# A gated cross-attention and FFN block on one Trainium2 core: FFN statistics one block earlier, first normalising on GpSimd, row loads in four pieces, two ScalarE roundings in other places

## The chip, the cores and the metric

The kernel runs on one core of a Trainium2 chip. The metric is the device time of one execution in microseconds (us). Three executions of the kernel before took 907.96, 905.91 and 907.97 us; the median is 907.96 us.

The engines are named as the profile names them: PE (TensorE, matrix products; PEld is its weight load), DVE (VectorE), ACT (ScalarE), POOL (GpSimd), and SP (SyncE), whose queue SPq issues nearly all DMAs. Each engine works through its own list of instructions in order and waits on semaphores.

## The reference

```python
x = x + tanh(g_xattn) * attention(layernorm(x), ctx, ctx, Wq, Wk, Wv, Wo)   # 16 heads of 32, causal mask
x = x + tanh(g_ffn)   * ffn(layernorm(x), w_gate, w_up, w_down)
# attention: softmax(q k^T / sqrt(32) + mask) v, then Wo; x is (2, 2048, 512), ctx is (2, 77, 512)
# ffn: (silu(x w_gate^T) * (x w_up^T)) w_down^T, hidden size 1536, integer weights / 127
# layernorm has no gain or bias, eps 1e-5
```

All of it is float32. The kernel splits each float32 operand of most products into a rounded high part (made by ACT) and a low part (the rest, made by DVE or POOL by a subtraction) and adds the cross products.

## The kernel before

**Stage 1, attention.** The 4096 rows are 8 blocks (n = 0 to 7) of 4 tiles (t = 0 to 3) of 128 rows. `step(n, ...)` exists once for each engine and states its order in a block. For tile t, PE computes the scores `scores(n, t)` in two halves; DVE's `shift` takes the maxima (L1029, L1037), subtracts (L1032) and scales (L1039); ACT takes exponentials, `exp0` (L767) for the first half and `exp1` (L774, eight pieces) for the second; DVE makes the denominators (L1052, L1054, L1058); POOL's `probabilities` (L571) multiplies by them. PE transposes the result, `p(t, 0)` to `p(t, 2)` (L1494), ACT rounds each transpose to its high part (L745) and DVE takes the low part (L998), which frees the PSUM bank. The second half of `scores(n, t+1)` waits for `exp1(n, t)`. `values` (L1460, psum<-pT,V) and the output projection `o(t)` (L1460, psum<-wo,aT) of the block before, and the query product `q(m)` of the next one (psum<-xT,wq), stand between these steps; `q(m)` may begin once DVE has freed one of two banks, by `q_low` (L1014). DVE's `residual` (L1064) ends a tile; SP writes it to the tensor `x_mid` (L404).

In block 0 alone, SP scatters the values of both batches into `v_full` with 24 small DMAs (L429), ACT rounds batch 0 in `v_high(0)` and batch 1 in `v_high(1)` (L736), and POOL and DVE make the low parts. ACT goes on to block 1 when `v_split[1]` has come, POOL's low part of batch 1.

For block n+1, SP spreads the factor `rstd` over partitions by two DMAs, one behind the other (`spread_rstd`: L359 writes `rs_row`, L365 reads `rsb`); POOL then scales (`x_scale`, L557) and takes the low parts (L563).

**To stage 2.** The FFN reads `x_mid` in 4 pairs of blocks, each 8 tiles of 128 x 512 in `x2`. For the first pair DVE computes mean and variance, `stats2` (L1116, L1118): 4 tiles in block 6 and 4 tiles in block 7. There, at the same place `st(t)` of each t: st(0) and st(1) do two tiles each, st(2) and st(3) call `normalise2` (L1124) for four tiles each. POOL's `rstd_ahead` (L651, L653) gives the factors. PE transposes the eight tiles in four `turn`s (L1572): B11 and B12 in block 7 after `o(3)`, ahead of `p(3, 0)`; B22 and B21 among the last `values`. ACT and DVE turn these into seven left factors of a Strassen product.

SP loads `x2` for the first pair as two DMAs of 1 MB (`load_x2`, L369), one before `residual(6)` and one after it. `residual(6)` also holds the `x_res` loads (L395) and `spread_rstd(7)`.

**Stage 2, FFN.** Each pair p has MH = 12 slices m of the hidden size (i = 12p + m). A slice is seven products of 4 matmuls: PE runs p1(i), p2(i), p4(i-1), p6(i), p3(i-1), p5(i), p7(i), 28 matmuls (L1705). After slice m = 6, PE runs the first half of the down products (`down`, 96 matmuls, L1755), and the second half after m = 11. Weights come in a ring of three slots: at the end of p3(i), SP issues `load_w(i+3)` (L387, 896 KB). In the first pair it first waits until DVE has taken the largest weight of the slot (L1345). Where other loads stand behind `load_w`, they and their waits delay the next `load_w`, since SP works in order.

ACT in slice m runs `snap1(i)` (L905, copy of p1, which p6(i) waits for), tanh2, tanh1, `snap2(i)` (L911), `h_high(i-1, 0)`, `snap3(i)` (L917), `h_high(i-1, 1)` (L937). `h_high(i-1, 1)` waits for DVE's `hidden2(i-1)` (L1332). POOL takes the low parts in `h_low` (L680). In the first pair POOL also converts the down weights (`convert`, L686), two of six pieces after each of `h_low(0)` to `h_low(2)`.

Other loads of SP in stage 2: pieces 4 and 5 of the down weights at m = 0 of the first pair; `acc` (the rows to which the result is added, 2 x 1 MB) at m = 2 of the first pair, behind a wait for all six conversions (L481), and at m = 0 of the others (L456); `x2` of the next pair (2 x 1 MB) at m = 3.

Of the kernel before, what the change touches and what calls it, by code (L numbers as in the profile page):

```python
# [5 lines left out]
def flamingo_gated_block(  # L6
# [31 lines left out]
    ALU = mybir.AluOpType  # L38
# [3 lines left out]
    P = 128  # L42
# [9 lines left out]
    TT = 4  # L52
# [55 lines left out]
    with ctx:  # L108
# [28 lines left out]
        rstd2 = sb("rstd2", [P, PT])  # L137

# [125 lines left out]
        acc_in = sem("acc_in")  # L264
        bn2_done, stats2_ready = sem("bn2_done"), sem("stats2_ready")
        var2_eps, rstd2_ready = sem("var2_eps"), sem("rstd2_ready")
        x2_normed = sem("x2_normed")
# [69 lines left out]
        def _(sp):  # L337
# [29 lines left out]
            def load_x2(q, j):  # L367

                sp.dma_start(x2[:, j * TT:(j + 1) * TT, :], mid_f[2 * q + j]).then_inc(x2_in[j], 16)  # L369
# [70 lines left out]
            load_x2(0, 0)  # L440
            residual(NB - 2, spread=True, keeps=((True,), (False,)))
            load_x2(0, 1)
# [9 lines left out]

            def load_rows(p):
                sp.wait_ge(out_done, 16 * PT * p)
                for j in range(2):
                    sp.dma_start(acc[:, j * TT:(j + 1) * TT, :], mid_f[2 * p + j]).then_inc(acc_in, 16)  # L456
# [7 lines left out]
            def pair(p):  # L464
                for m in range(MH):
                    i = MH * p + m
                    sp.wait_ge(p3_full, i + 1)
                    if p == 0 and m < HH:
                        sp.wait_ge(w_max_done, m + 1)
                    if p == NP - 1 and m >= HH:  # L470
                        sp.wait_ge(w_max_done, m + 1)
                    if i + 3 < MH * NP:
                        load_w(i + 3)
                    if p == 0 and m == 0:
                        for j in (4, 5):
                            sp.wait_ge(rd_used, j - 3)
                            load_down(j)
                    if p == 0 and m == 2:
                        sp.wait_ge(rd_used, HH)
                        for j in range(2):  # L480
                            sp.dma_start(acc[:, j * TT:(j + 1) * TT, :], mid_f[j]).then_inc(acc_in, 16)  # L481
                    if p > 0 and m == 0:
                        load_rows(p)
                    if p + 1 < NP and m == 3:
                        sp.wait_ge(xb_full, nth(TURNED, p, B21))
                        for j in range(2):
                            load_x2(p + 1, j)
                for t in range(PT):
                    sp.wait_ge(m_free, M_P2 + 16 * p + 9 + t)
                    sp.dma_start(out_f[2 * p + t // TT, :, t % TT, :], acc[:, t, :]).then_inc(out_done, 16)  # L490
# [21 lines left out]
        def _(pool):  # L512
# [201 lines left out]
        def _(act):  # L714
# [83 lines left out]
            def step(n, first, query):  # L798
# [31 lines left out]
                if first:  # L830
# [4 lines left out]
                    v_high(1)  # L835
# [4 lines left out]
                    q(2)  # L840
                    p(3, 0)
# [97 lines left out]
            def pair(p, more):  # L939
                last = MH * p + MH - 1  # L940
                for m in range(MH):
                    i = MH * p + m
                    snap1(i)
                    if m:
                        tanh2(i - 1)
                        tanh1(i - 1)
# [4 lines left out]
                    if m:  # L951
                        h_high(i - 1, 1)
# [27 lines left out]
        def _(dve):  # L980
# [130 lines left out]
            def stats2(i, t):  # L1111

                at = TT * (i % 2) + t
                if t == 0:
                    dve.wait_ge(x2_in[i % 2], 16 * (i // 2 + 1))
# [36 lines left out]
            def step(n, first, query, ahead):  # L1152
# [181 lines left out]
            def result(p, h, t):  # L1334
                dve.wait_ge(m_full, M_P2 + 16 * p + PT * h + t + 1)
                if h == 0:
                    dve.wait_ge(acc_in, 32 * (p + 1))
# [118 lines left out]
        def _(pe):  # L1456
# [88 lines left out]
            def turn(q, j):  # L1545
# [4 lines left out]
                pe.wait_ge(x2_normed, PT * q + TT * (half_of + 1))  # L1550
# [300 lines left out]
```

## Time and profile before

| | |
|---|---|
| median of 3 executions | 907.96 us |
| the profiled execution | 910.43 us, of which 908.6 us are its span |
| PE busy | 865.1 us, 95% of the span |
| DVE, ACT, POOL busy | 643.1, 435.8, 427.5 us |
| DMA | 129.53 MB, mean 143 GB/s |
| stage 1, stage 2 | to about 403 us, from about 403 us |

In the timeline a row is: start in us, time in us, engine, line, operation, output <- inputs, shapes, count of instructions, and in brackets the engine's idle time just before and what ended it. Neighbours of the same kind are merged into one row. A matmul lasts longer than the distance to the next (they are pipelined), so the pace of PE is read from the time of a whole row. PEclk is the share of full clock that PE was granted: 1.00 is 2.4 GHz, 0.50 is 1.2 GHz.

### The profile page before, as it was taken

The page shows a single profiled execution, that of the slowest core. Times are in us where ns is not written, and L with a number is a line of the kernel's source. Part 1 is how long each engine was busy: PE and PEld are TensorE (multiplying, and loading weights), DVE is VectorE, ACT ScalarE, POOL GpSimd, SP SyncE. Part 2 cuts the span into 40 slices and gives each one's busy share as a digit, 9 for nine tenths or more (in the row PEclk, how much of TensorE's full clock was granted, in tenths as well). Part 3 has the DMA queues.
Part 4 walks back from the last instruction along what each step waited for, and adds up shares of the span by engine and source line. Part 5 has one row for each costly group of instructions (what it writes and reads, how often), then busy time and mean ns, then how long its engine had stood idle before and what let it go on. Part 6 is the DMA issues. An engine that isn't in the chain of part 4 may idle for free.

```text
span 908.6 us, 12903 instructions
## 1 busy us (share of the span) xinstructions
PE 865.1 (95%) x4089; PEld 712.7 (78%) x4089; DVE 643.1 (71%) x1090; ACT 435.8 (48%) x1130; POOL 427.5 (47%) x362
## 2 busy tenths in 40 slices
PE   4978999999999999899899999999999999999997
PEld 2757888888888887678688888888888878888876
DVE  3776868685868778759668747687567677477682
ACT  2565656555565656436406536246355165362450
POOL 5364767675767663146414524334534145242240
PEclk9999999999999999899999999999999999999999
DMA  6425373655546350526804327324256043262212
GB/s 199 151 61 177 114 232 128 195 163 161 176 153 218 116 207 12 203 73 235 307 0 144 135 86 275 126 82 157 93 202 233 2 158 119 97 219 79 82 41 94
DMA packets 61589, 129.53 MB, mean 143 GB/s; under 512 B 8416, under 2 KB 21216, under 8 KB 61536
## 3 DMA queue, kind: packets, MB, share of 16 engines
q1 hardware_dynamic: 61248, 128.85, 41.5%
q8 instruction: 29, 0.48, 0.2%
q14 instruction: 24, 0.20, 0.1%
q10 hardware_dynamic: 288, 0.00, 0.0%
HBM read 100.72 MB, written 27.80 MB: 141 GB/s over the span
## 4 chain that ended last, share of the span: by engine, by line
PE 76%; DVE 7%; POOL 5%; ACT 4%; issue 3%; SPq 3%; DMA 2%; ACTq 0%; POOLq 0%; DVEq 0%
PE psum L1705 30%; PE psum L1460 24%; PE psum L1755 18%; POOL xs L557 3%; PE psum L1494 3%; SPq L429 2%; POOL e L571 1%; DMA ring<-w_var 1%; POOL hT L680 1%; PE psum L1572 1%; ACT e L774 1%; DVE pT L998 1%; DVE x L1124 1%; DMA wq_stage<-wq_t 1%; ACT pT L745 1%
## 5 line engine op out<-in xcount | busy, mean ns | idle before, releaser
L1705 PE MATMUL psum<-xv,ring 128*128 128x512 f32 x1344 | 310.3, 392 | 5.1 <-DMA ring<-w_var 3.6
L1705 PEld LDWEIGHTS psum<-xv,ring 128*128 128x128 f32 x1344 | 252.1, 189 | 60.8 <-issue 4.2
L680 POOL TENSOR_TENSOR hT<-th,hT 128x512 fp32r<-128x512 f32 x48 | 85.1, 1772 | 221.0 <-ACT hT L937 221.0
L1755 PE MATMUL psum<-w_d,hT 128*128 128x512 f32 x768 | 177.6, 390 | 1.2 <-POOL hT L680 0.7
L1755 PEld LDWEIGHTS psum<-w_d,hT 128*128 128x128 f32 x768 | 143.6, 188 | 32.5 <-POOL hT L680 2.0
L571 POOL TENSOR_TENSOR e<-e,rden 128x616 f32<-128x616 f32 x64 | 77.9, 1217 | 115.2 <-DVE rden L1054 83.7
L1460 PE MATMUL psum<-xT,wq 128*128 128x512 f32 x384 | 96.5, 405 | 3.0 <-POOL xT L563 2.9
L1460 PE MATMUL psum<-wo,aT 128*128 128x512 f32 x384 | 95.1, 398 | 0.5 <-DVE aT L1014 0.5
L1340 DVE SCALAR_TENSOR_TENSOR acc<-psum,gate_ffn,acc 128x512 f32<-128x512 f32 x64 | 47.6, 749 | 65.5 <-PE psum L1755 65.4
L905 ACT ACTIVATE a<-psum 128x512 f32<-128x512 f32 x48 | 28.3, 590 | 125.6 <-PE psum L1705 125.6
L1460 PEld LDWEIGHTS psum<-xT,wq 128*128 128x128 f32 x384 | 72.4, 194 | 18.3 <-POOL xT L563 3.1
L1460 PEld LDWEIGHTS psum<-wo,aT 128*128 128x128 f32 x384 | 69.9, 188 | 14.4 <-DVE aT L1014 0.8
L774 ACT ACTIVATE e<-psum,nmx 128x77 f32<-128x77 f32 x256 | 79.1, 338 | 0.2 <-DVE nmx L1039 0.2
L745 ACT ACTIVATE pT<-psum 128x512 fp32r<-128x512 f32 (+1 forms) x96 | 50.4, 533 | 45.4 <-PE psum L1494 45.4
L1460 PE MATMUL psum<-pT,V 128*128 128x512 f32 x288 | 67.9, 393 | 0.0
L680 POOL TENSOR_TENSOR hT<-c,hT 128x512 fp32r<-128x512 f32 x48 | 62.3, 1297 | 11.2 <-ACT hT L937 11.2
L1460 PE MATMUL psum<-K,qT 128*128 128x308 f32 x384 | 65.0, 313 | 2.3 <-ACT e L774 1.9
L998 DVE TENSOR_TENSOR pT<-psum,pT 128x512 fp32r<-128x512 f32 (+1 forms) x96 | 55.9, 588 | 14.3 <-ACT pT L745 13.3
L1460 PEld LDWEIGHTS psum<-pT,V 128*128 128x128 f32 x288 | 54.2, 190 | 11.0
L1460 PEld LDWEIGHTS psum<-K,qT 128*128 128x128 f32 x384 | 57.1, 188 | 7.0 <-ACT e L774 2.7
L1494 PE MATMUL psum<-ident,e 128*128 128x128 f32 x320 | 48.8, 282 | 11.3 <-DVE pT L998 10.3
L1299 DVE TENSOR_TENSOR c<-psum,a 128x512 f32<-128x512 f32 x48 | 33.0, 689 | 34.0 <-ACT a L917 34.0
(105 smaller groups left out, 1220.7 us busy)
## 6 DMA issues: line engine op xcount, KB each, us to landing
ring<-w_var SPq DMA_DIRECT2D x48, 896.0 KB, 4.8
w_var<-stage SPq DMA_DIRECT2D x12, 896.0 KB, 5.0
x_ln<-x SPq DMA_DIRECT2D x32, 256.0 KB, 4.7
x_res<-x SPq DMA_DIRECT2D x32, 256.0 KB, 6.3
x_mid<-x_res SPq DMA_DIRECT2D x32, 256.0 KB, 2.0
x<-x_mid SPq DMA_DIRECT2D x8, 1024.0 KB, 8.9
acc<-x_mid SPq DMA_DIRECT2D x8, 1024.0 KB, 8.2
out<-acc SPq DMA_DIRECT2D x32, 256.0 KB, 2.0
```

Source lines behind the costliest of these rows:

```text
L571: nc.gpsimd.tensor_tensor(e[:, t % 2, hs], e[:, t % 2, hs], rden[:, t % 2, hs].unsqueeze(2).to_broadcast([P, UH, SK]), ALU.mult).then_inc( ...
L680: nc.gpsimd.tensor_tensor(hT[:, 1, i % HH, j, :], h[:, :], hT[:, 0, i % HH, j, :].bitcast(f32), ALU.subtract).then_inc(h_lo, 1)
L745: nc.scalar.activation(dst, src, ACT.Copy).then_inc(t_hi, 1)
L774: last = nc.scalar.activation(e[:, t % 2, UH + h, :], s_bank[1][:, h // HG, (h % HG) * SK:(h % HG + 1) * SK], ACT.Exp, bias=nmx[:, t % 2, ...
L905: nc.scalar.activation(a1[:, :], psum[:, set_a[i % 2], :], ACT.Copy).then_inc(a1_done, 1)
L998: nc.vector.tensor_tensor(dst, src, hi.bitcast(f32), ALU.subtract).then_inc(t_free, 1)
L1299: nc.vector.tensor_tensor(c22[:, :], psum[:, set_c[i % 2], :], a3[:, :], ALU.add).then_inc(c22_done, 1)
L1340: nc.vector.scalar_tensor_tensor(acc[:, t, :], m_bank[t % 2][:, :], gate_ffn[:, 0:1], acc[:, t, :], ALU.mult, ALU.add).then_inc(m_free, 1)
L1460: last = nc.tensor.matmul(dst, stat, mov, start=(j == 0), stop=(j == len(terms) - 1))
L1494: last = nc.tensor.transpose(t_bank[at % 2][:, j * P:(j + 1) * P], rows[:, start:start + P], ident[:, :])
L1705: last = nc.tensor.matmul(psum[:, bank, :], stat, mov, start=start and j == 0, stop=j == len(terms) - 1, skip_group_check=not start)
L1755: last = nc.tensor.matmul(m_bank[t % 2][:, :], hT[:, a, m, t // TT, (t % TT) * P:(t % TT + 1) * P], w_d[:, HH * h + m, :], start=m == 0 an ...
```

## The change

- SP: `x2` comes in four pieces of 512 KB (2 tiles each). For the first pair all four are issued ahead of `residual(6)`. For the others one piece stands behind `load_w` at each of m = 0 to 3. `acc` also comes in four pieces, one at m = 4 and three at m = 5, each with its own semaphore; the waits for `out_done` and for the conversions move to m = 4. Pieces 4 and 5 of the down weights move from m = 0 to m = 1.
- DVE: in block 6 `st(t)` computes statistics of two tiles (8 in all); in block 7 it does nothing.
- POOL: both `rstd_ahead` stand before `probabilities(7, 0)`, and `normalise_first` (a negated mean, then four tiles by (x - mean) * rstd) stands after `probabilities(7, 0)` and after `probabilities(7, 1)`.
- ACT: `v_high(1)` moves from after `p(2, 0)` of block 0 to after `q(2)`. `h_high(i-1, 1)` moves from the end of slice i to after `snap1(i+1)`, except in slices 6 and 11, where it stays.

```diff
-            def load_x2(q, j):
-                sp.dma_start(x2[:, j * TT:(j + 1) * TT, :], mid_f[2 * q + j]).then_inc(x2_in[j], 16)
+            def load_x2(q, i):
+                sp.dma_start(x2[:, 2 * i:2 * i + 2, :], mid_f[2 * q + i // 2, :, 2 * (i % 2):2 * (i % 2) + 2, :])\
+                    .then_inc(x2_in[i // 2], 16)
+            def load_acc(p, i):
+                sp.dma_start(acc[:, 2 * i:2 * i + 2, :], mid_f[2 * p + i // 2, :, 2 * (i % 2):2 * (i % 2) + 2, :])\
+                    .then_inc(acc_in[i], 16)
...
-            load_x2(0, 0)
+            for i in range(TT):
+                load_x2(0, i)
             residual(NB - 2, spread=True, keeps=((True,), (False,)))
-            load_x2(0, 1)
             residual(NB - 1, keeps=((False,), ()))
...
-                    if p == 0 and m == 0:
+                    if p == 0 and m == 1:
                         for j in (4, 5):
                             sp.wait_ge(rd_used, j - 3)
                             load_down(j)
-                    if p == 0 and m == 2:
-                        sp.wait_ge(rd_used, HH)
-                        for j in range(2):
-                            sp.dma_start(acc[:, j * TT:(j + 1) * TT, :], mid_f[j]).then_inc(acc_in, 16)
-                    if p > 0 and m == 0:
-                        load_rows(p)
-                    if p + 1 < NP and m == 3:
+                    if p + 1 < NP and m < TT:
                         sp.wait_ge(xb_full, nth(TURNED, p, B21))
-                        for j in range(2):
-                            load_x2(p + 1, j)
+                        load_x2(p + 1, m)
+                    if m == TT:
+                        if p:
+                            sp.wait_ge(out_done, 16 * PT * p)
+                        else:
+                            sp.wait_ge(rd_used, HH)
+                        load_acc(p, 0)
+                    if m == TT + 1:
+                        for j in range(1, TT):
+                            load_acc(p, j)
...
+            def normalise_first(i):
+                c = slice(TT * i, TT * i + TT)
+                nc.gpsimd.tensor_scalar(nmean2[:, c], mv2[:, c, 0], -1.0, 0.0, ALU.mult, ALU.add).then_inc(nmean_ready, 1)
+                pool.wait_ge(nmean_ready, i + 1)
+                pool.wait_ge(rstd2_ready, i + 1)
+                for t in range(TT):
+                    at = TT * i + t
+                    nc.gpsimd.tensor_scalar(x2[:, at, :], x2[:, at, :], nmean2[:, at:at + 1], rstd2[:, at:at + 1],
+                                            ALU.add, ALU.mult).then_inc(x2_normed0, 1)
+            rstd_ahead(0)
+            rstd_ahead(1)
             probabilities(NB - 1, 0)
-            rstd_ahead(0)
+            normalise_first(0)
             probabilities(NB - 1, 1)
+            normalise_first(1)
             probabilities(NB - 1, 2)
-            rstd_ahead(1)
             probabilities(NB - 1, 3)
...
                     p(2, 0)
-                    v_high(1)
                     p(2, 1)
                     exp1(n, 3)
                     q(1)
                     p(2, 2)
                     q(2)
+                    v_high(1)
                     p(3, 0)
...
                     snap1(i)
+                    if m > 1 and m != HH + 1:
+                        h_high(i - 2, 1)
                     if m:
                         tanh2(i - 1)
...
                     snap3(i)
-                    if m:
+                    if m in (HH, MH - 1):
                         h_high(i - 1, 1)
...
                     elif query:
-                        stats2(0, t)
-                    elif t < 2:
-                        stats2(1, 2 * t)
-                        stats2(1, 2 * t + 1)
-                    else:
-                        normalise2(t - 2)
+                        stats2(t // 2, 2 * (t % 2))
+                        stats2(t // 2, 2 * (t % 2) + 1)
```

The other lines of the diff give `acc` four semaphores, let PE's first `turn`s wait for `x2_normed0`, and fit the counts of the waits.

## Rows read from the trace of the kernel before

**Rows 1.** The page: busy time by engine, with counts of instructions.

```profile
PE 865.1 (95%) x4089; PEld 712.7 (78%) x4089; DVE 643.1 (71%) x1090; ACT 435.8 (48%) x1130; POOL 427.5 (47%) x362
```

**Rows 2.** Waits of PE, whole span: engine, line, releaser: us, times, longest.

```profile
PE psum L1572 <- DVE x L1124: 3.3, 2, 2.6
```

**Rows 3.** Timeline, block 0, ACT, POOL and PE.

```profile
68.50 1.49 ACT L736 ACTIVATE V<-v_full 128x1536 fp32r<-128x1536 f32 x1 [1.88 <-DMA v_full<-v_keys]
...
74.41 3.46 POOL L600 TENSOR_TENSOR V<-v_full,V 128x1536 fp32r<-128x1536 f32 x1
...
74.61 1.08 PE L1494 MATMUL psum<-ident,e 128*128 128x128 f32 x4 [2.05 <-DVE pT L998]
75.35 4.22 PE L1460 MATMUL psum<-xT,wq 128*128 128x512 f32 x12
...
81.94 8.35 PE L1460 MATMUL psum<-pT,V 128*128 128x512 f32 x36
```

**Rows 4.** Timeline, block 6, SP, POOL, DVE, PEld and PE.

```profile
298.47 0.33 SPq L365 DMA_DIRECT2D rsb<-rs_row  x1
...
305.08 5.03 POOL L557 TENSOR_TENSOR xs<-xs,rsb 128x512 f32<-128x512 f32 x4
...
319.43 0.68 DVE L998 TENSOR_TENSOR pT<-psum,pT 128x512 fp32r<-128x512 f32 x1
...
320.17 0.36 PEld L1494 LDWEIGHTS psum<-ident,e 128*128 128x128 f32 x2
...
328.81 5.72 PE L1460 MATMUL psum<-xT,wq 128*128 128x512 f32 x24
...
329.99 0.66 DVE L1014 TENSOR_TENSOR qT<-psum,qT 128x512 fp32r<-128x512 f32 x1
```

**Rows 5.** The tile rsb from 286 to 310 us: time from issue to landing.

```profile
DMA to landing us min/median/max: 3.5/3.5/3.5
```

**Rows 6.** Timeline, block 7, POOL, DVE, PE.

```profile
344.69 1.22 POOL L571 TENSOR_TENSOR e<-e,rden 128x616 f32<-128x616 f32 x1 [7.47 <-DVE rden L1054]
...
355.73 0.69 DVE L1116 BATCH_NORM_STATS2 bn<-x 128x6 f32<-128x512 f32 x1
...
357.35 0.78 DVE L1029 TENSOR_REDUCE mx<-psum 128x8 f32<-128x616 f32 x1
...
361.55 1.22 POOL L571 TENSOR_TENSOR e<-e,rden 128x616 f32<-128x616 f32 x1 [4.93 <-DVE rden L1054]
...
368.41 3.01 PE L1460 MATMUL psum<-wo,aT 128*128 128x512 f32 x12
...
372.10 1.09 PE L1572 MATMUL psum<-ident,x 128*128 128x128 f32 x8 [0.69 <-DVE x L1124]
...
375.82 1.97 PE L1572 MATMUL psum<-ident,x 128*128 128x128 f32 x8 [2.62 <-DVE x L1124]
...
380.39 4.96 PE L1460 MATMUL psum<-pT,V 128*128 128x512 f32 x18
```

**Rows 7.** Windows: us; busy and count of PE, PEld, DVE, ACT, POOL; PEclk, DMA share, GB/s.

```profile
375.00:378.00 3.00, 2.18 (x10) 2.19 (x11) 1.89 (x3) 0.00 (x0) 0.00 (x0) 0.50 0.94 326
```

**Rows 8.** One line each: L549 (first block's normalising on POOL); L1039 on DVE.

```profile
L549 POOL TENSOR_SCALAR x_ln<-x_ln,nmean,rstd x4: 767/767/768, 10.8 to 13.0; 128x512 f32<-128x512 f32 x4
L1039 DVE TENSOR_SCALAR nmx<-mx x32: 171/172/1052, 40.8 to 367.4; 128x8 f32<-128x8 f32 x32
```

**Rows 9.** Timeline, first pair: SP, then PE.

```profile
433.72 0.45 SPq L387 DMA_DIRECT2D ring<-w_var  x1
...
443.38 8.14 PE L1705 MATMUL psum<-xv,ring 128*128 128x512 f32 x28 [3.64 <-DMA ring<-w_var]
```

**Rows 10.** Chain in order of time: a stretch of the first pair without stops.

```profile
473.29 31.75 PE psum L1705 x140
```

**Rows 11.** The tile ring, whole span: time from issue to landing.

```profile
DMA to landing us min/median/max: 4.3/4.8/12.8
```

**Rows 12.** Timeline, third pair, PE at p6 of slice 8.

```profile
731.13 3.03 PE L1705 MATMUL psum<-xv,ring 128*128 128x512 f32 x12 [0.77 <-ACT a L905]
```

More of the change, by code:

```diff
@@ L137, in flamingo_gated_block @@
         rstd2 = sb("rstd2", [P, PT])
+        nmean2 = sb("nmean2", [P, PT])
         with ExitStack() as a0:
@@ L263, in flamingo_gated_block @@
         x2_in = [sem(f"x2_in{i}") for i in range(2)]
-        acc_in = sem("acc_in")
+        acc_in = [sem(f"acc_in{i}") for i in range(4)]
         bn2_done, stats2_ready = sem("bn2_done"), sem("stats2_ready")
         var2_eps, rstd2_ready = sem("var2_eps"), sem("rstd2_ready")
-        x2_normed = sem("x2_normed")
+        x2_normed0, x2_normed, nmean_ready = sem("x2_normed0"), sem("x2_normed"), sem("nmean_ready")
         p1_full, p2_full, p3_full, p4_full, p5_full, p6_full, p7_full = (sem(f"p{i}_full") for i in range(1, 8))
@@ L451, in _ @@
                 sp.wait_ge(mid_out[t], 16 * NB)
-            def load_rows(p):
-                sp.wait_ge(out_done, 16 * PT * p)
-                for j in range(2):
-                    sp.dma_start(acc[:, j * TT:(j + 1) * TT, :], mid_f[2 * p + j]).then_inc(acc_in, 16)
             def load_down(i):
@@ L477, in pair @@
                             load_down(j)
-                    if p == 0 and m == 2:
-                        sp.wait_ge(rd_used, HH)
-                        for j in range(2):
-                            sp.dma_start(acc[:, j * TT:(j + 1) * TT, :], mid_f[j]).then_inc(acc_in, 16)
-                    if p > 0 and m == 0:
-                        load_rows(p)
-                    if p + 1 < NP and m == 3:
-                        sp.wait_ge(xb_full, nth(TURNED, p, B21))
-                        for j in range(2):
-                            load_x2(p + 1, j)
+                    if p + 1 < NP and m < TT:
+                        sp.wait_ge(xb_full, nth(TURNED, p, B21))
+                        load_x2(p + 1, m)
[8 more added lines that the diff above has]
+                            load_acc(p, j)
                 for t in range(PT):
@@ L1114, in stats2 @@
                 if t == 0:
-                    dve.wait_ge(x2_in[i % 2], 16 * (i // 2 + 1))
+                    dve.wait_ge(x2_in[i % 2], 32 * (i // 2 + 1))
                 nc.vector.bn_stats(bn2[:, at, :], x2[:, at, :]).then_inc(bn2_done, 1)
@@ L1336, in result @@
                 if h == 0:
-                    dve.wait_ge(acc_in, 32 * (p + 1))
+                    dve.wait_ge(acc_in[t // 2], 16 * (p + 1))
                 else:
@@ L1549, in turn @@
                 last_i = MH * q - 1
-                pe.wait_ge(x2_normed, PT * q + TT * (half_of + 1))
+                if q:
+                    pe.wait_ge(x2_normed, PT * (q - 1) + TT * (half_of + 1))
+                else:
+                    pe.wait_ge(x2_normed0, TT * (half_of + 1))
                 if j == B11:
```

## Prediction

> **What bounds the kernel.** I read the page first: PE is busy for 865.1 of 908.6 us [rows 1], so only two things can change the time much: where PE stands still, and where it works at a lower clock. So next the waits of PE, then the granted clock window by window, then the timeline around each wait. The wait list is misleading if read alone: it has 3.3 us for the transposes of `x2` behind normalising [rows 2], but after some stops PE is also slower for a while. Four places bear on this change.
>
> Block 0: ACT stands at `v_high(1)` until a DMA lands at 68.50, and `exp1(0, 3)`, the four `q` and `p` roundings are queued behind it [rows 3]. Block 7: two tiles of statistics stand directly in front of `shift(2)`, on which the tile's exponentials wait; later PE waits for `normalise2`, and its clock is 0.50 just after [rows 6, 7]. First pair: a weight load is issued at 433.72 behind `acc` and its wait, PE stands for 3.64 us and then takes 8.14 us for 28 matmuls [rows 9], where 140 take 31.75 us elsewhere [rows 10], that is 6.35 us for 28. Third pair: p6 of slice 8 waits 0.77 us for `snap1` [rows 12].
>
> **Block 0, `v_high(1)` moved: 3.4 us won.** ACT waited 1.88 us, from 66.62 to 68.50, and worked to 69.99 [rows 3]; without both, `p(2, 1)` and `exp1(0, 3)` come 3.3 us sooner. `v_high(1)` now fits behind `q(2)`, at about 72.7 to 74.2; POOL's low part of it, which stood behind `probabilities(0, 3)` until 74.41 [rows 3], begins no later, and nobody waits for it before block 1. PE was done with `q(2)` and `p(3, 0)` at 74.61 - 2.05 = 72.56, stood, and took 4.22 us for the 12 matmuls of `q(3)` [rows 3], where 12 take 3.01 us in block 7 [rows 6]. After, `p(3, 1)` (0.5 us) and `q(3)` (3.0 us) follow at once and end at 76.1; `p(3, 2)` and the scores, whose second half waits for DVE to free `q(3)` (ACT 0.6 us, DVE 0.7 us), let `values` begin at about 78.5 instead of 81.94 [rows 3]. If the slow pace remains, 1.2 us and one more piece of it are lost: the low end is 1.9, the high end 3.5.
>
> **Block 6, four more tiles of statistics on DVE: 1.5 us lost.** Two tiles take 357.35 - 355.73 = 1.62 us [rows 6], and four more are 3.3 us, in four places of 0.8 us. DVE has hardly a gap there. In front of `shift(2)`: the low part of `p(1, 0)` ends at 320.1, and PE's `p(1, 2)` is loaded at 320.17 [rows 4], so 0.8 us go straight to PE. `q_low(0)`, which ends at 330.65, comes behind three of the four places and is 2.5 us late, at 333.15; `q(2)`, the second half of 5.72 us from 328.81 [rows 4], would begin at 331.67 and is 0.8 late already, so it waits 0.7 us more. Behind that DVE waits for ACT and catches up. Sum about 1.5. The bounds: 0 if the chain of exponentials hides it, 3.3 if all of it shows.
>
> **Block 6, 1 MB more ahead of `rs_row`: nothing, but close.** `rsb` is issued at 298.47 [rows 4] and lands 3.5 us later [rows 5], at 302.0; POOL begins to scale at 305.08 [rows 4], so the slack is 3.1 us. Another 1 MB at the 326 GB/s of a busy window [rows 7] is 3.2 us. I take 0 and up to 1.5 us as a bound; the cover is `probabilities(6, 0)`. The three more DMA issues, each under 0.5 us of SP's time, lie inside the backlog that these bytes make.
>
> **Block 7: 5.6 us won.** On POOL, both `rstd_ahead` go into a 7.47 us gap before `probabilities(7, 0)`. `normalise_first` is 4 x 0.767 [rows 8] plus 0.2 for the mean, 3.3 us: the first lies between `probabilities(7, 0)` and `(7, 1)`, where POOL is as idle, the second in a gap of 4.93 us [rows 6], now some 1.5 us shorter, so it just fits. On DVE, `shift(2)` starts 1.5 us sooner, `shift(3)` nearly 3. PE then is the later one: `o(1)`, `p(1, 2)`, the scores, `p(2, 0)`, `p(2, 1)`, `o(2)`, `p(2, 2)`, `o(3)` run close together, and `o(3)` ends at about 370.4, not 371.4 [rows 6]. `turn` B11 needs 1.09 us, and B12, which began at 375.82 behind 2.62 us of waiting and took 1.97 us [rows 6], now follows it: 372.6. `p(3, 0)` and `p(3, 1)` end at 373.7; ACT has B11's copy (1.0 us) ahead of rounding them, PE waits 0.9 us, and `values` begins at 375.0 instead of 380.39 [rows 6], 5.4 us sooner. Its first 18 matmuls took 4.96 us [rows 6] and at 2.4 GHz would take 4.4: 0.6 more. POOL's normalising runs beside DVE's scaling of the second maxima (L1039), which is 0.17 us alone and was up to 1.05 us in blocks where POOL is busy [rows 8]; it is on the chain once, and I take off 0.4. Bounds: 2.5 if DVE's chain stays the later one and the clock falls as before; 6.5.
>
> The Trainium skill ("SBUF — State Buffer", Who interferes with whom) says that GpSimd and VectorE share a port pair that one of them holds for a whole instruction, the other blocking fully. The maximum of L1039 agrees in kind [rows 8]. By that rule a collision costs at most one 0.767 us instruction of POOL, so the block would win 5.6 + 0.4 - 0.8 = 5.2 us, and the sum would be 13.3.
>
> **First pair of stage 2: 5.4 us won.** The wait for the conversions and the 2 MB of `acc` no longer stand before `load_w(6)`. It is issued at the end of p3(3), about 431.3, and lands after about 4.8 us [rows 11], at 436; p1(6) comes at 439.7. The stop of 3.64 and the slow 8.14 - 6.35 = 1.79 go together. Pieces 4 and 5 of the down weights come one slice later: about 425, needed by POOL at 430. The row pieces stand behind `load_w` and have a slice of 6.35 us before the next: 896 + 512 KB in 6.35 us is 227 GB/s, below the 326 seen. `acc` is asked for at about 438 and 444 and used from 449. Bounds: 3.6 (the slow pace stays elsewhere) and 5.5.
>
> **`h_high`: 0.8 us won.** `snap1(8)` of the third pair no longer waits for `hidden2` behind the long DVE stretch [rows 12]. In ordinary slices p6 has 1.8 us of cover (8 matmuls) and the rounding lies in front of tanh2, which is then 0.5 us later with as much slack; POOL's low part ends 1 us ahead of the next use. Bounds 0 and 0.8.
>
> **Sum.** 3.4 - 1.5 + 0 + 5.6 + 5.4 + 0.8 = 13.7 us. Against the profiled execution, 910.43 us, this gives 896.7; that one stands 2.5 above the median of 907.96, so the predicted median is 894.3 us.
>
> **Rivals.** (a) The waits go, the clock does not come back. PE still stands for 2.9 us in block 0 and has short stops in block 7, and low stretches may fall on other work. For it: at 375 to 378 the clock was 0.50 though the stop just before was only 2.62 us [rows 6, 7], and three of my terms count on full pace. Against: the stops that preceded those stretches go. Price: 1.2 in block 0; in block 7 0.6 for the first `values`, 1.97 - 1.09 = 0.9 for B12 and some 0.5 for the `p(3, ...)` behind it; 1.8 in the first pair. That is 5.0 us, so 8.7 are won: 899.3.
>
> (b) Block 6 is dearer: all of the 3.3 us of statistics shows and `rsb` lands 1.5 us late, against 1.5 in my sum. Price 3.3 more: 897.6. For it: DVE hardly idles there, and the slack is within 0.1 us of the extra load. Against: ACT and PE have some slack of their own behind `q(2)`.
>
> (c) Slower: the row pieces hold up the ring in every pair. A load has 36 matmuls, 8.2 us, from issue to use. If pieces of 512 KB move so slowly that one is still in the queue when the next `load_w` is issued, and a load passes 8.2 us once in each of the four pairs, each costs what it cost in the first pair, 3.64 + 1.79 = 5.4 us. The win outside that pair is 8.3, so the net is 4 x 5.4 - 8.3 = 13.3 us slower, 921.3. The point from which it decides is the second stop in all: 2 x 5.4 is more than the 8.3 won elsewhere. Against it: the median landing is 4.8 us, and the one load that made PE stop stood behind 2 MB and a wait [rows 9, 11]. The Trainium skill ("DMA: Bandwidth & Descriptors", Rules for kernel authors) advises at least 1 MiB per DMA for bandwidth and so speaks for this rival; no row here shows halves to be slower than wholes.
>
> (d) The change does not do what it says: `normalise_first` lags on POOL and holds `probabilities(7, 2)`, so that block 7 gives only 2.5. Price 3.1: 897.4.
>
> **Chances.** Forecast 0.55 (891.5 to 896.5), (a) 0.15, (b) 0.13, (d) 0.10, (c) 0.03, and 0.04 for something that brings the time to within 0.3% of before, which is about what a measurement of this kernel can tell from no change (2.7 us). The range is 890.5 to 902.0: it holds the forecast, (a), (b), (d) and most pairs of them. Faster 0.93, same 0.04, slower 0.03.
>
> **What would show it.** Right: no wait of PE L1705 for the ring; no `L1572` wait for DVE; `values` of block 1 some 3.4 us sooner; stage 2 beginning about 7.5 us sooner (3.4 - 1.5 + 5.6); PEclk 1.00 between the turns and `values`, and in slice 6 of the first pair. In block 6, PE waiting for L998 or L1014 about 1.5 us. Wrong: POOL waiting for `rsb`; `probabilities(7, 2)` directly behind normalising; new low stretches of PEclk; landings of ring loads above 8 us.

## The result and the profile after

The changed kernel takes 893.96 us (median of 4 executions, 893.72 to 894.10) against 907.97 us for the kernel before on the same chip (4 executions, 905.91 to 908.66). The ratio is 0.9847, with a 95% interval of 0.9835 to 0.9859: 14.0 us less. The forecast was 894.3.

The profiled execution after took 893.84 us, that before 910.43, so the two profiles differ by 16.6 us, not 14.0. That gap turns out to matter.

The page after, busy time by engine:

```profile
span 892.0 us, 12923 instructions
PE 858.7 (96%) x4089; PEld 708.5 (79%) x4089; DVE 655.2 (73%) x1082; ACT 439.6 (49%) x1130; POOL 437.0 (49%) x372
```

PE is busy 6.4 us less for the same 4089 matmuls [rows 1]: that is pace (clock), not work. DVE is busy 12 us more, though it lost the normalising of the first pair.

Waits of PE after, whole span (engine, line, releaser: us, times, longest; the first matmuls' load and lines below 0.5 us left out):

```profile
PE psum L1509 <- DVE pT L1017: 8.4, 9, 1.3
...
PE psum L1475 <- DVE qT L1033: 0.7, 2, 0.5
```

The ring's wait and the waits of the `x2` transposes (now L1590) for DVE are not in that list. The four places, one after the other.

**Block 0.** Timeline after, ACT, then PE:

```profile
72.45 1.48 ACT L753 ACTIVATE V<-v_full 128x1536 fp32r<-128x1536 f32 x1
...
71.76 1.03 PE L1509 MATMUL psum<-ident,e 128*128 128x128 f32 x8
72.55 3.02 PE L1475 MATMUL psum<-xT,wq 128*128 128x512 f32 x12
...
77.94 2.23 PE L1475 MATMUL psum<-pT,V 128*128 128x512 f32 x9
```

`p(3, 0)` is whole, without the stop in its middle, `q(3)` takes 3.02 us, and `values` begin 4.0 us sooner than in [rows 3].

**Block 6.** POOL's scaling from 296 to 304 us after (the tile `xs`: durations in ns, first and last start):

```profile
L561 POOL TENSOR_TENSOR xs<-xs,rsb x3: 1289/1291/1292, 301.3 to 303.8; 128x512 f32<-128x512 f32 x3
```

And the timeline after, PE:

```profile
317.16 0.44 PE L1509 MATMUL psum<-ident,e 128*128 128x128 f32 x2 [0.43 <-DVE pT L1017]
...
329.32 3.02 PE L1475 MATMUL psum<-xT,wq 128*128 128x512 f32 x12 [0.49 <-DVE qT L1033]
```

POOL begins at 301.3, 3.8 us sooner than in [rows 4], so `rsb` did not hold it. PE waits for DVE's rounding of `p` and `q`, and the last rows of the block are only 2.2 us sooner: the block lost 1.6 us.

**Block 7.** Timeline after, POOL, then DVE, then PE:

```profile
354.68 3.04 POOL L680 TENSOR_SCALAR x<-x,nmean,rstd 128x512 f32<-128x512 f32 x4
357.84 1.22 POOL L575 TENSOR_TENSOR e<-e,rden 128x616 f32<-128x616 f32 x1
...
347.50 0.79 DVE L1048 TENSOR_REDUCE mx<-psum 128x8 f32<-128x616 f32 x1
353.53 0.79 DVE L1048 TENSOR_REDUCE mx<-psum 128x8 f32<-128x616 f32 x1
...
363.90 3.02 PE L1475 MATMUL psum<-wo,aT 128*128 128x512 f32 x12
366.76 1.91 PE L1590 MATMUL psum<-ident,x 128*128 128x128 f32 x16
...
371.02 4.36 PE L1475 MATMUL psum<-pT,V 128*128 128x512 f32 x18
```

A tile now takes 6.03 us (353.53 - 347.50), where it took 7.65 before (from 349.70 to 357.35 [rows 6]). Between 353.88 and 366.76 PE has no wait. Before, the same stretch had three (timeline, PE, before):

```profile
360.59 0.44 PE L1494 MATMUL psum<-ident,e 128*128 128x128 f32 x2 [0.52 <-DVE pT L998]
...
362.77 1.12 PE L1460 MATMUL psum<-K,qT 128*128 128x308 f32 x6 [0.89 <-ACT e L774]
...
368.21 0.44 PE L1494 MATMUL psum<-ident,e 128*128 128x128 f32 x2 [0.49 <-DVE pT L998]
```

Normalising is ready (357.72) long before PE turns `x2` at 366.76, both halves in one go, and `values` begin at 371.02 instead of 380.39 [rows 6]; the 18 matmuls take 4.36 us, not 4.96. Windows after, over the turns and what follows (us; busy and count of PE, PEld, DVE, ACT, POOL; PEclk, DMA share, GB/s), where [rows 7] had 0.50:

```profile
366.00:371.00 5.00, 3.72 (x31) 3.26 (x30) 2.80 (x4) 2.88 (x4) 0.47 (x1) 1.00 0.54 179
371.00:378.00 7.00, 7.00 (x37) 5.89 (x37) 4.43 (x6) 2.67 (x5) 0.00 (x0) 1.00 1.00 411
```

**First pair.** The chain in order of time after (start, us):

```profile
392.96 42.81 PE psum L1723 x188
435.77 21.77 PE psum L1773 x96
```

The timeline of SP's queue after:

```profile
433.98 0.34 SPq L394 DMA_DIRECT2D ring<-w_var  x1
434.36 1.90 SPq L375 DMA_DIRECT2D acc<-x_mid  x3
```

The three pieces of `acc` stand behind the weight load. And the tile `ring` after, from issue to landing:

```profile
DMA to landing us min/median/max: 4.4/4.6/8.2
```

All 188 up matmuls of half a pair run as one stretch, as they did before in the later pairs. The down matmuls begin at 435.77 instead of 451.52, 15.75 us sooner, where stage 2 itself begins 10.0 sooner (392.96 against 402.96): 5.75 us won inside the pair.

**Last pair.** It runs from 764.86 to 887.22, 122.36 us; before it took 121.90. Half a microsecond was lost there, which no step of the prediction has. The third pair is 1.1 us shorter (125.07 before, 123.97 now). Together the places account for the two profiles: 4.0 - 1.6 + 7.8 + 5.8 + 1.1 - 0.5 = 16.6 us.

### The profile page after: what moved, and what is told of

It reads as the page before. It is cut to its first block, busy times and chain, and to the rows that moved or that the text cites. A ratio compares the mean times of both kernels' runs of the same rounds, so it can differ in the third digit from the quotient of the medians.

```text
span 892.0 us, 12923 instructions
## 1 busy us (share of the span) xinstructions
PE 858.7 (96%) x4089; PEld 708.5 (79%) x4089; DVE 655.2 (73%) x1082; ACT 439.6 (49%) x1130; POOL 437.0 (49%) x372
## 4 chain that ended last, share of the span: by engine, by line
PE 79%; POOL 6%; DVE 6%; ACT 4%; issue 3%; DMA 1%; SPq 0%; ACTq 0%; POOLq 0%; DVEq 0%
PE psum L1723 34%; PE psum L1475 24%; PE psum L1773 18%; POOL xs L561 4%; PE psum L1509 3%; POOL e L575 2%; ACT e L791 1%; PE psum L1590 1%; ACT pT L762 1%; DMA wq_stage<-wq_t 1%; DVE pT L1017 1%; DVE den L1071 1%; POOL hT L697 1%; DVE aT L1033 1%; ACT aT L779 1%
## 5 line engine op out<-in xcount | busy, mean ns | idle before, releaser
L1319 DVE SCALAR_TENSOR_TENSOR th<-th,c 128x512 f32<-128x512 f32 x48 | 56.1, 1168 | 7.1 <-ACT th L947 4.3
L954 ACT ACTIVATE hT<-th 128x512 fp32r<-128x512 f32 x48 | 30.4, 633 | 54.2 <-DVE th L1332 54.2
```

The costliest lines, as they stand in the source:

```text
L954: nc.scalar.activation(hT[:, 0, i % HH, j, :], h[:, :], ACT.Copy).then_inc(h_hi, 1)
L1319: nc.vector.scalar_tensor_tensor(th2[:, :], th2[:, :], 1.0, c22[:, :], ALU.add, ALU.mult)\
```

## The experiments

Twelve runs, one of them (9) the kernel before again. "Before" and "after" are the two kernels of this document. Times are medians; each ratio is against the kernel before on the same chip.

**1 to 4: the parts one at a time.** Four edits of the kernel before, each taking one part of the change. My theory: the terms of the sum. The rival: the parts lean on each other, so that they do not add up.

Only `v_high(1)` moved:

```diff
                     p(2, 0)
-                    v_high(1)
                     p(2, 1)
...
                     q(2)
+                    v_high(1)
```

> The kernel before with one edit: v_high(1) of block 0 stands after q(2). My theory: ACT's wait for the last of the v_full DMAs and the rounding itself held exp1(0,3), and the slow pace of q(3) came from the stop behind it, so values of block 1 begins 3.4 to 4.0 us sooner than at 81.94 and nothing gives it back: 3.4 to 4.0 us faster. Rival: the slow pace of q(3) stays wherever the stop goes, 1.9 to 2.5 us faster. Second rival: the gain is given back at the start of stage 2, 0 to 1 us faster.

Measured: 905.71 us, 0.9978 (0.9969 to 0.9986), 2.3 us won (1.3 to 2.8), less than the 3.4 of the sum. The number is that of the first rival (1.9 to 2.5), but not for its reason: in this trace `q(3)` takes 3.00 us, so its slow pace did not stay. Experiment 9 has the reason.

Only `h_high(., 1)` moved:

```diff
                     snap1(i)
+                    if m > 1 and m != HH + 1:
+                        h_high(i - 2, 1)
...
-                    if m:
+                    if m in (HH, MH - 1):
                         h_high(i - 1, 1)
```

> The kernel before with one edit: h_high(i-1, 1) stands after snap1(i+1), as in the changed kernel. My theory: only the 0.77 us wait of p6 in slice 8 of the third pair goes: 0.8 us faster, and no other wait of L1705 appears. Rival: tanh2 that is now later delays PE in the pairs where DVE is full (first and last): same or up to 0.5 us slower.

Measured: 908.64 us, 1.0012 (1.0003 to 1.0020): 0.6 us lost by the medians (0.3 to 1.8 by the interval) where 0.8 were to be won. In its trace the third pair is 1.1 us shorter, as wanted; but the first pair is 1.0 longer and the last 0.4. Timeline of the last pair, DVE and POOL, this kernel:

```profile
858.37 0.68 DVE L1292 TENSOR_TENSOR c<-psum,a 128x512 f32<-128x512 f32 x1
858.51 1.30 POOL L680 TENSOR_TENSOR hT<-c,hT 128x512 fp32r<-128x512 f32 x1 [0.63 <-ACT hT L937]
859.15 1.20 DVE L1306 SCALAR_TENSOR_TENSOR th<-th,c 128x512 f32<-128x512 f32 x1
```

The same operation, `silu2`, grouped by line, in the kernel before (count, busy us, mean ns, idle time before):

```profile
L1304 DVE SCALAR_TENSOR_TENSOR th<-th,c 128x512 f32<-128x512 f32 x48 | 36.0, 751 | 4.6 <-ACT th L930 4.3
```

and in this one:

```profile
L1306 DVE SCALAR_TENSOR_TENSOR th<-th,c 128x512 f32<-128x512 f32 x48 | 56.0, 1168 | 7.1 <-ACT th L930 4.3
```

The earlier rounding lets POOL begin its `h_low` earlier, and it now lies across DVE's `silu2`, which reads only SBUF. That operation takes 1.20 us instead of 0.68, ending 0.5 us after POOL's; the one just before, which reads PSUM, overlaps POOL's too and still takes 0.68. The changed kernel has the same mean of 1168 ns: 48 x 0.42 is 20 us, and less the 4.5 of normalising that left and some 3 of other operations that POOL now crosses less, this is DVE's 12 us of extra busy time. The Trainium skill ("SBUF — State Buffer", Who interferes with whom) says that a DVE instruction with two SBUF inputs contends with a GpSimd instruction that reads SBUF, and that one with at most one SBUF input, outside certain modes, does not. The trace agrees on both, with 0.5 us a time for the first.

The first pair's loss is another chain. Waits of SP's queue from 383 to 450 us, this kernel:

```profile
SPq L481 <- POOL w_d L686: 8.4, 1, 8.4
```

The same of the kernel before, from 395 to 450 us:

```profile
SPq L481 <- POOL w_d L686: 7.4, 1, 7.4
```

And this kernel's wait of PE for the ring:

```profile
PE psum L1707 <- DMA ring<-w_var: 4.5, 2, 4.1
```

POOL takes `h_low` ahead of a conversion of the down weights, SP waits longer for the conversions in front of `load_w`, and the ring's wait grows from 3.6 to 4.5 us.

Only SP's queue of stage 2 (places and 512 KB pieces):

```diff
-                    if p == 0 and m == 2:
-                        sp.wait_ge(rd_used, HH)
...
+                    if p + 1 < NP and m < TT:
...
+                        load_x2(p + 1, m)
+                    if m == TT:
...
+                        load_acc(p, 0)
```

> The kernel before with the loads of stage 2 placed as in the changed kernel, in pieces of 512 KB; the first pair's x2 comes in four pieces, two of them ahead of residual(6) and two behind it, so that block 6 has the same bytes in its queue as before. My theory: the wait for the ring and the slow 28 matmuls behind it go, 5.4 us faster in the profile. Rival a: the slow pace stays, 3.6. Rival b: the ring is late in other slices, 2 us or less, or slower. Rival c: in most executions of the kernel before the stop is followed by no slow stretch, then the median moves by 3.6 only, while its profile shows what the first theory says.

Measured: 902.60 us, 0.9938 (0.9925 to 0.9950), 5.4 us won (4.5 to 6.8). Its chain in order of time:

```profile
403.00 43.14 PE psum L1710 x188
```

The stop and the slow 28 matmuls are gone together; the first pair takes 124.3 us instead of 129.8.

Only blocks 6 and 7 changed (statistics, normalising on POOL, the early `x2` loads; SP's places of stage 2 as before, but in 512 KB pieces):

> The changed kernel with v_high(1) and h_high back in their old places and the loads of stage 2 at their old places (in pieces of 512 KB): only blocks 6 and 7 are changed. By the two profiles block 6 costs 1.6 us and block 7 with the start of stage 2 wins 7.8: 6.2 us faster, with the ring's stop of 3.6 us still there. By my recorded terms 5.6 - 1.5 = 4.1 us faster. Rival: without the other parts the clock falls in block 7 all the same: 3 us or less.

Measured: 901.36 us, 0.9931 (0.9916 to 0.9946), 6.7 us won (4.9 to 7.6), against 5.6 - 1.5 = 4.1 of the sum. The second profile of the kernel before (experiment 9) has `values` of block 0 at the same time (79.39, here 79.37), so the two can be compared: stage 2 begins 6.2 us sooner here (394.33 against 400.55), and the third pair is 1.0 us shorter (124.03 against 125.00). That the third pair is shorter was not expected, since `h_high` is in its old place here. Timeline of the third pair, POOL and DVE, in the kernel before, which waits at [rows 12]:

```profile
728.09 1.29 POOL L680 TENSOR_TENSOR hT<-th,hT 128x512 fp32r<-128x512 f32 x1 [5.51 <-ACT hT L937]
728.42 1.51 DVE L1332 TENSOR_TENSOR c<-c,th 128x512 f32<-128x512 f32 x1 [0.47 <-DVE c L1325]
```

and in this one, which does not:

```profile
718.82 0.69 DVE L1345 TENSOR_TENSOR c<-c,th 128x512 f32<-128x512 f32 x1
718.86 1.81 POOL L697 TENSOR_TENSOR hT<-th,hT 128x512 fp32r<-128x512 f32 x1 [5.51 <-ACT hT L954]
```

So the wait at [rows 12] is the same kind of collision, and who comes first decides. Where POOL does (before twice, experiments 1, 2, 3 and 7), `hidden2` (L1332) takes 1.51 us; where DVE is 0.04 us ahead (after, and the other experiments), it takes 0.69 and POOL pays instead, with 1.81 for 1.29. What tips it one way or the other no run here shows. In experiments 2 and 7 POOL comes first and PE still doesn't wait: there the rounding is moved, so `snap1` no longer stands behind `hidden2`. Either is enough.

Together: 2.3 - 0.6 + 5.4 + 6.7 = 13.8, against 14.0 for the whole change. But this doesn't show that the parts add up. The microsecond of the third pair is in experiment 2 and in experiment 4, and can be won only once; the microsecond that experiment 2 lost in the first pair isn't lost in the whole change (its first pair takes 124.01 us, 0.3 less than experiment 5 without the early rounding there), where the ring's stop is gone. The parts do lean on each other, in two places that cancel.

**5: `h_high` where it helps.** In the kernel after, the early rounding at slice 8 alone, which is where [rows 12] shows its use:

```diff
-                    if m > 1 and m != HH + 1:
+                    if m == HH + 2:
                         h_high(i - 2, 1)
...
-                    if m in (HH, MH - 1):
+                    if m and m != HH + 1:
                         h_high(i - 1, 1)
```

> The changed kernel, but h_high(i-1, 1) goes back to the end of its slice everywhere except that h_high(6, 1) of each pair still stands behind snap1 of slice 8. In the changed kernel DVE's silu2 (one SCALAR_TENSOR_TENSOR with both inputs in SBUF) takes 1168 ns on average instead of 751, because POOL's low part of h now runs beside it, and the last pair, where DVE is full, takes 0.46 us longer. My theory: both go back, silu2 to 750 ns, the third pair keeps its gain: 0.3 to 0.8 us faster than the changed kernel. Rival: the last pair is longer for another reason, silu2 goes back and the time does not: within 0.2 us.

Measured: 893.84 us, 0.9846 (0.9833 to 0.9858), no different from the change. `silu2` is back at a mean of 799 ns, and the last pair takes 121.86 us, 0.5 less; but the first takes 0.3 more (188 matmuls in 43.11 us, not 42.81). DVE's time is mostly hidden, and what it cost at the end the early rounding roughly gives back in the first pair. That slice 8 still needs it is not shown: `hidden2` takes 0.69 us there in this kernel and after, as in experiment 4, which has no wait without it.

**6: the statistics of block 6 in other places.** After, with one tile per `st(t)` and the other four behind `q(1)` and `p(3, 0)` of DVE's list:

```diff
                     elif query:
-                        stats2(t // 2, 2 * (t % 2))
-                        stats2(t // 2, 2 * (t % 2) + 1)
+                        stats2(0, t)
...
                     q(1)
+                    if query and not ahead:
+                        stats2(1, 0)
+                        stats2(1, 1)
                     q(2)
                     p(3, 0)
+                    if query and not ahead:
+                        stats2(1, 2)
+                        stats2(1, 3)
```

> The changed kernel with the four added tiles of statistics of block 6 moved from st(0) to st(3) to two places where DVE waits for ACT: two behind q(1), two behind p(3, 0). My theory: what block 6 lost (1.6 us by the two profiles) was DVE's low part of p(1, 0) and its q_low(0) coming late; PE then no longer waits at these places and 1.3 to 1.6 us are won on the changed kernel, unless the statistics end too late for POOL's rstd_ahead. Rival: the loss was the later load of rsb or the clock, then nothing is won. Second rival: it moves to block 7, 0 to 0.5 us won.

Measured: 892.16 us, 0.9828 (0.9815 to 0.9841), 1.8 us better than the change. Timeline of block 6, DVE, then PE, this kernel:

```profile
328.36 0.68 DVE L1135 BATCH_NORM_STATS2 bn<-x 128x6 f32<-128x512 f32 x1
...
330.47 0.69 DVE L1033 TENSOR_TENSOR qT<-psum,qT 128x512 fp32r<-128x512 f32 x1 [0.42 <-ACT qT L779]
...
324.07 5.74 PE L1480 MATMUL psum<-xT,wq 128*128 128x512 f32 x24
```

Here DVE still idles 0.42 us behind the statistics, where it waits for ACT, and PE takes its 24 matmuls of `q(1)` and `q(2)` in one stretch, without the 0.49 us seen above. So the 1.5 us of the prediction's block 6 were real, and avoidable.

**7: who normalises.** After, with DVE normalising the first pair in block 7 (in `st(2)` and `st(3)`, as before), and all statistics in block 6:

```diff
                         stats2(t // 2, 2 * (t % 2) + 1)
+                    elif t >= 2:
+                        normalise2(t - 2)
...
-            normalise_first(0)
             probabilities(NB - 1, 1)
-            normalise_first(1)
```

> The changed kernel, but the first pair is normalised by DVE in block 7 again, at st(2) and st(3); the statistics stay in block 6. This separates the two halves of what block 7 won. My theory: the statistics were in series with every tile (about 1.5 us each for two tiles, 3 us), and the normalising stood in front of both turns (0.7 and 2.6 us of waiting) with the slow stretch behind them, so that 3 to 5 us of the 7.8 come back as loss: 897 to 899 us. Rival: the normalising hides once DVE is early, loss below 1 us. Other rival: the statistics alone were hidden by PE and all comes from normalising, loss of 6 to 8 us.

Measured: 896.94 us, 0.9879 (0.9865 to 0.9893), 3.0 us worse than the change. The wait comes back. Timeline of block 7, PE, this kernel:

```profile
371.07 1.50 PE L1576 MATMUL psum<-ident,x 128*128 128x128 f32 x8 [2.62 <-DVE x L1130]
...
375.10 4.38 PE L1464 MATMUL psum<-pT,V 128*128 128x512 f32 x18
```

So of the 6.2 us that the trace of experiment 4 has for blocks 6 and 7, 3.0 come from normalising on POOL, and the rest, some 3, from taking the statistics out of block 7, net of what they cost in block 6.

**8 and 10: size or place.** Two edits of the kernel after. First, transfers of 1 MB at the change's places (`x2` at m = 1 and 3, `acc` at m = 4 and 5):

```diff
-                        load_x2(p + 1, m)
+                        if m % 2:
+                            load_x2(p + 1, m // 2)
...
-                        for j in range(1, TT):
-                            load_acc(p, j)
+                        load_acc(p, 1)
```

> The changed kernel with x2 and acc in whole transfers of 1 MB: x2 of the first pair as two ahead of residual(6), of the others at m = 1 and m = 3 behind load_w, acc at m = 4 and m = 5. My theory: what counted was the place of acc and its wait, not the size: no ring wait comes back, within 0.5 us of the changed kernel. Rival: the size counts, a load_w behind 1 MB lands more than 8.2 us after its issue and PE waits once or more, 2 us slower or worse.

Measured: 893.65 us, 0.9843 (0.9831 to 0.9856), the same as with 512 KB. The ring's landing, this kernel:

```profile
DMA to landing us min/median/max: 4.3/4.6/8.5
```

Second, the pieces of 512 KB at the places of before (`acc` at m = 2 behind the wait for the conversions, `x2` at m = 3):

> The changed kernel with the loads of stage 2 at the places of the kernel before (down weights 4 and 5 at m = 0, acc and its wait at m = 2 in the first pair and m = 0 later, all four pieces of x2 at m = 3), still in pieces of 512 KB. My theory: the ring's stop of about 3.6 us comes back in slice 6 of the first pair, with a slow stretch behind it in some executions only: 3.6 to 5.4 us slower than the changed kernel. Rival: the other parts have shifted the work so that the stop is gone anyway: within 1 us.

Measured: 900.97 us, 0.9917 (0.9904 to 0.9931), 7.0 us worse than the change, more than the theory or its rival gave. Timeline of SP's queue, this kernel:

```profile
424.74 1.92 SPq L375 DMA_DIRECT2D acc<-x_mid  x4
426.75 0.41 SPq L394 DMA_DIRECT2D ring<-w_var  x1
```

Its chain in order of time, behind the stop:

```profile
435.47 9.43 PE psum L1723 x28
```

Its waits, of PE over the whole span and of SP's queue from 383 to 450 us:

```profile
PE psum L1723 <- DMA ring<-w_var: 5.4, 2, 4.4
...
SPq L375 <- POOL w_d L703: 9.0, 1, 9.0
```

Counted from the start of stage 2, this `load_w(6)` comes at 426.75 - 393.34 = 33.4 us; before, it came at 433.72 - 402.96 = 30.8 [rows 9]. One microsecond of the 2.6 is issuing four pieces instead of two ahead of it (1.92 us against 0.93), the rest the longer wait for POOL's conversions (9.0 against 7.4). That rest belongs to the early rounding, as in experiment 2: in experiment 4, with the same pieces at the same places and the rounding where it was, the wait is 7.4 us, and PE stops for 3.2 us. Here PE stands 5.4 us in all and takes 9.43 us for the next 28 matmuls, 3.1 more than at full pace; this profiled execution, 903.51 us, is again 2.5 above its median. So the place is worth the whole term (5.4 us in the kernel before, 7.0 here), the size nothing at good places, and at the old place small pieces only add issue time.

**12: `v_high(1)` put back** in the kernel after, the edit of 1 reversed.

> The changed kernel with v_high(1) of block 0 back after p(2, 0). Alone on the kernel before, the move won 2.3 us by the medians though its place in the trace moved by 4.0 us in the changed kernel. My theory: PE's stop in front of it costs 2.0 us always and the slow pace behind it 1.4 to 1.7 us only where a low stretch falls there, so 2 to 3.5 us are lost here too, with low stretches in block 0 that differ between executions. Rival: what was won alone was partly given back at the start of stage 2, and is lost in full here: 3.5 to 4.0.

Measured: 895.69 us, 0.9858 (0.9843 to 0.9873): the move is worth 1.7 us in the kernel after, below the 2 to 3.5 expected, 2.3 in the kernel before, 3.4 in neither.

**9: the kernel before, profiled again.** The question: how much of the 16.6 us between the two profiles belongs to the one execution that I read?

> The kernel before, unchanged, profiled once more. Its execution in the first profile took 910.43 us against medians of 907.7 to 908.0, and the sum of my terms was made against it. My theory: the low stretches of PEclk fall differently from execution to execution, each worth about 1.7 us of PE's work, so that this profile has another set of them and, apart from them, the same waits of PE. Rival: the set is the same and the spread comes from DMA or from the start of the program.

Measured: 907.14 us. Timeline of block 0, PE, this execution:

```profile
73.34 0.63 PE L1494 MATMUL psum<-ident,e 128*128 128x128 f32 x4 [1.02 <-DVE pT L998]
73.72 3.02 PE L1460 MATMUL psum<-xT,wq 128*128 128x512 f32 x12
...
79.39 4.94 PE L1460 MATMUL psum<-pT,V 128*128 128x512 f32 x21
```

The DMA that `v_high(1)` waits for landed a good microsecond sooner (ACT began at 67.2, not at 68.50), PE stopped for 1.02 us instead of 2.05, and `q(3)` ran at full pace, 3.02 us instead of 4.22. `values` begin at 79.39, not at 81.94 [rows 3]: 2.55 us less. That accounts for most of the 3.3 us between the two executions, and is as much as the profiled execution stood above the median. Experiment 3, whose profiled execution took 905.10 us, also 2.5 above its median, has the same place late (81.80). The same place in the kernels with `v_high(1)` in its old place (before twice, experiments 2, 3, 4 and 12) reads 81.94, 79.39, 80.13, 81.80, 79.37 and 79.61, mean 80.4; with it moved (after, experiments 1, 5, 6, 7, 8, 10 and 11) 77.23 to 78.92, mean 78.1. The difference of means is 2.2 us.

**11: the best of both.** After, with the statistics as in experiment 6 and the early rounding in the first pair and at slice 8 only.

> The changed kernel with two edits: the statistics of block 6 placed where DVE waits (as in the run that did this alone, 1.8 us faster), and h_high(i-1, 1) moved only in the first pair and in slice 8 of the others. My theory: the first pair keeps its 0.3 us, the last pair gets back its 0.5 us, and the two edits add up: 2.1 to 2.5 us faster than the changed kernel, about 891.7. Rival: they do not add up, 892.2 or more.

Measured: 892.11 us, 0.9821 (0.9807 to 0.9834), the same as experiment 6. From the start of stage 2 to the end it is 0.9 us shorter than there, of which 0.5 lie in the last pair, but stage 2 begins 0.9 later (391.41 against 390.47), with no edit in stage 1 that could do it; nearly all of that is there in block 0 already (`values` at 78.08 against 77.23). Five executions can't settle half a microsecond; whether this placing of `h_high` is worth anything stays open.

## Why the prediction was right, and where it was not

The forecast of 894.3 us is 0.3 us from the measured 893.96, but three of its terms were off by more than a microsecond and cancelled. What was to happen in each place did happen, except for `h_high`; that the sum came so close is luck.

- **`v_high(1)`, 3.4 predicted, 1.7 to 2.3 measured.** The mechanism was right. The size came from an execution in which the DMA landed late and `q(3)` ran slowly, and the step that failed is taking both the term from that execution and 2.5 us off for its place above the median: most of those 2.5 us were this very place (2.55 us between the two profiles of the kernel before), and so were counted twice. Against its own profile the change won 4.0 us here; against a typical execution, some 2. The low end, 1.9, was the honest value. I had the hint, since I said that the profile stood 2.5 above the median, and did not ask where.
- **Block 6, 1.5 lost, predicted and found:** 1.6 in the trace, and 1.8 come back when the statistics go elsewhere. PE's waits are those named. The other half of the step, `rsb`, cost nothing, as forecast; but it was near. It was issued at 297.13, landed after 3.5 us at 300.6, and POOL began at 301.3.
- **Block 7, 5.6 predicted, 7.8 found.** This is the term with the wrong size. The turns without waiting and the 0.6 us of clock were right (4.9 and 0.6 found, against 4.4 and 0.6, the 0.4 for contention taken off in the sum). The step that failed is "PE then is the later one, and `o(3)` ends at about 370.4, not 371.4", 1.0 us sooner. In fact it ended at 366.9, 2.3 sooner beyond the 2.2 that block 6 passed on. That PE is the later one was right, as it has no wait from 353.88 to 366.76; what was too small was the 1.0 us, since three waits of 0.52, 0.89 and 0.49 us went. The prediction doesn't show how it sized PE's share. I had added up the durations of PE's rows for a tile, which is too long: each row ends with the tail of its last matmul, over which the next row already runs (354.88 + 2.98 = 357.86, while the next begins at 357.70), and with five or six rows to a tile that is most of a microsecond each time. The contention term of 0.4 did not show either: L1058, behind the second maximum, took 0.27 us once in block 7 beside normalising and 0.17 otherwise. Blocks 6 and 7 together: 4.1 predicted, 6.2 in the trace of experiment 4.
- **First pair, 5.4 predicted, 5.4 measured alone,** 5.75 in the trace: stop and slow pace went together, and no new wait came. Putting the places back in the kernel after costs more, 7.0, for the reason given in experiment 10.
- **`h_high`, 0.8 won predicted, 0.6 lost measured alone.** The third pair's wait went (1.1 us), but its cause was only half seen: `hidden2` was late because POOL's `h_low` lay across it (1.51 us for 0.69), and in the changed kernel DVE comes first there, so that the wait would probably have gone without the move, as in experiment 4. The move does keep PE from waiting where POOL comes first (experiments 2 and 7). The step that failed is "in ordinary slices p6 has 1.8 us of cover ... with as much slack": I asked what follows on ACT and PE, but not what POOL's `h_low`, coming earlier, would lie beside (DVE's `silu2`) and in front of (the conversions that SP waits for). In the changed kernel the second can't hurt, since the ring's loads no longer stand behind those conversions; the first costs 0.46 us in the last pair.

Of the rivals, (a) did not come: there is no low stretch behind the former stops. For (b), block 6 cost what was forecast. (c) was tried from both sides by experiment 8 and by the change, whose slowest ring load took 8.2 us, with no stop. The advice of the Trainium skill ("DMA: Bandwidth & Descriptors", Rules for kernel authors) that transfers be at least 1 MiB for the highest bandwidth made no difference to the time here: 893.65 us with 1 MB, 893.96 with 512 KB. (d) did not come either, but its sign did: `probabilities(7, 2)` stands 0.1 us behind normalising (357.84 behind 357.72). It was not late, since DVE's `rden` was ready only at 357.75. So POOL has nothing left there.

## What to carry to other kernels

Before sizing a term from a profile, find out where the profiled execution differs from the median: if that is the place the change touches, the offset and the term are the same microseconds. In a queue, the order decides: a load that the bound engine needs next must stand in front of every wait for something else, and then the size of the others matters little. And of a step that is moved earlier, ask what its consumer, now earlier too, will lie beside.

## What the runs showed of the hardware

- A DVE operation with both inputs in SBUF went from 0.68 to 1.20 us beside a POOL operation of 1.30 us that had begun first, ending 0.5 us behind it. With DVE 0.04 us ahead it was POOL's operation that went from 1.29 to 1.81 us. DVE operations reading PSUM were not longer beside POOL (0.68).
- After PE's stops of 1.0 to 1.2 us in block 0 (before again, experiments 4 and 12) `q(3)` took 3.02 us. After 2.05 us and 2.26 us (before, experiment 3) it took 4.2, at a granted clock of 0.68, and after 2.36 us (experiment 2) 3.00, at 1.00. So the clock does not always fall behind nearly the same stop.
- In the first pair, the 28 matmuls behind the ring's stop of 3.2 to 4.4 us took 8.0 to 9.4 us in five executions (granted clock 0.68 to 0.81), and 6.63 in one, at 1.00, whose stop was the shortest, 2.9 us (experiment 1). The time of one execution of this kernel carries one or two microseconds of such differences.
